# Source indices loaded once and copied into slots on chip, eight slots for gathered rows

## The reference

```
h  = relu(layernorm(x))
Q, K, V = h Wq + bq, h Wk + bk, h Wv + bv          (8 heads of 12)
Ee = edge_attr We + be
score(e) = exp(clip(sum over a head of K[src] * Q[dst] * Ee / sqrt(12), -5, 5))
x  = x + segsum(V[src] * score, dst) / (segsum(score, dst) + 1e-6)

h  = relu(layernorm(x))
m  = segsum(h[src], dst) / max(degree, 1)
y  = m Wl^T + bl + h Wr^T
x  = x + relu(batchnorm over all nodes(y))
```

## Time and profile before

| | |
|---|---|
| time, median of 3 runs | 4154.96 us (4154.8 to 4155.78) |
| span of the profiled execution | 5273.9 us |
| busy: PE, DVE, ACT, POOL | 2391.0, 1669.6, 365.5, 3049.5 us |
| gathers, stage 1 (L569) | 1564, mean 964 ns |
| gathers, stage 2 (L586) | 1564, mean 944 ns |

### The profile page before, as it was taken

The page is one execution under the profiler, slowest core; times in us unless marked ns, Lnnn a source line. Parts: engine busy times, 40 slices in busy tenths (PEclk is TensorE's granted clock), DMA queues, the critical chain, the costliest instruction groups (busy, mean ns, idle before and its releaser), DMA issues.

```text
span 5273.9 us, 63499 instructions
## 1 busy us (share of the span) xinstructions
PE 2391.0 (45%) x12016; PEld 2151.5 (41%) x12016; DVE 1669.6 (32%) x4551; ACT 365.5 (7%) x847; POOL 3049.5 (58%) x3199
## 2 busy tenths in 40 slices
PE   6555556555555565555553233333333333323332
PEld 4455555555555555555552222222222222222221
DVE  7344444444444444444442111111011111111114
ACT  5000100001000110001010000000000000000000
POOL 3555555555555555555554566665656666666564
PEclk9555555555555555555555555555555555555555
DMA  6444444444444444444441111111111111111112
GB/s 193 109 111 111 113 109 113 109 114 114 107 114 116 110 117 111 108 110 110 114 115 32 32 36 34 34 36 33 36 34 34 34 36 34 34 35 34 33 37 53
DMA packets 468836, 408.10 MB, mean 77 GB/s; under 512 B 279436, under 2 KB 380740, under 8 KB 468812
## 3 DMA queue, kind: packets, MB, share of 16 engines
q0 software_dynamic: 125120, 230.82, 18.8%
q1 hardware_dynamic: 317292, 164.73, 12.9%
q10 hardware_dynamic: 26400, 12.29, 0.8%
HBM read 380.19 MB, written 27.32 MB: 77 GB/s over the span
## 4 chain that ended last, share of the span: by engine, by line
another core or an unknown queue 34%; issue 22%; DVE 13%; DVEq 12%; PE 8%; DMA 4%; POOL 3%; SPq 2%; ACT 1%; POOLq 0%; ACTq 0%
DVEq L308 4%; DVE prod L1073 3%; POOL kvg L586 3%; DVEq L1011 3%; PE psum L667 3%; PE psum L751 2%; PE psum L676 2%; DMA kvg<-h_tab,idx 2%; DVE acc L1011 1%; DVE score L1078 1%; DMA idx<-in_src_dram 1%; DVE msg L1084 1%; DVE sel L1001 1%; DVE prod L1067 1%
## 5 line engine op out<-in xcount | busy, mean ns | idle before, releaser
L569 POOL DMA_INDIRECT kvg<-kv_tab,idx x1564 | 1507.7, 964 | 1142.4 <-issue 795.1
L586 POOL DMA_INDIRECT kvg<-h_tab,idx x1564 | 1476.3, 944 | 934.1 <-issue 502.4
L751 PE MATMUL psum<-sel,kvg 128*97 128x42 f32 x3136 | 583.2, 365 | 1382.4 <-DVE sel L1001 595.5
L751 PEld LDWEIGHTS psum<-sel,kvg 128*97 128x97 f32 x3136 | 533.2, 276 | 1454.4 <-issue 1066.7
L667 PE MATMUL psum<-sel,msg 128*104 128x42 f32 x3136 | 632.3, 381 | 789.6 <-DVE msg L1084 598.4
L667 PEld LDWEIGHTS psum<-sel,msg 128*104 128x104 f32 x3136 | 573.1, 288 | 869.5 <-DVE msg L1084 637.3
L1011 DVE TENSOR_TENSOR acc<-acc,psum 104x42 f32 (+1 forms) x784 | 156.2, 199 | 2423.4 <-remote 1433.7
L676 PE MATMUL psum<-we,ea_t 97*128 97x96 f32 x3136 | 837.1, 446 | 8.5 <-DMA ea_t<-in_edge_attr_dram 8.5
L676 PEld LDWEIGHTS psum<-we,ea_t 97*128 97x128 f32 x3136 | 771.8, 330 | 9.2 <-issue 9.2
L1067 DVE TENSOR_TENSOR prod<-kvg,psum 128x384 f32<-128x384 f32 x392 | 216.0, 551 | 566.8 <-remote 517.9
L683 PE MATMUL psum<-q_win,sel_t 126*128 126x96 bf16 x1568 | 202.7, 280 | 324.9 <-DVE sel_t L1056 199.1
(11 more groups left out here) (134 smaller groups left out, 1139.2 us busy)
## 6 DMA issues: line engine op xcount, KB each, us to landing
ea_t<-in_edge_attr_dram SPq DMA_DIRECT2D x392, 192.0 KB
dst_row<-rel_tab SPq DMA_DIRECT2D x392, 126.0 KB
kvg<-kv_tab,idx POOLq DMA_INDIRECT x1564
kvg<-h_tab,idx POOLq DMA_INDIRECT x1564
idx<-in_src_dram SPq DMA_DIRECT2D x782, 2.0 KB
kv_tab<-kvq_out SPq DMA_DIRECT2D x25, 384.0 KB, 2.5
q_win<-q_tab SPq DMA_DIRECT2D x392, 23.6 KB
q_tab<-q_out ACTq DMA_DIRECT2D x25, 288.0 KB, 2.4
```

What stands on the lines that cost most here:

```text
L569: pool.indirect_dma_start(out=kv_slot[k][:, t, :], out_offset=None, in_=kv_tab[:, :], in_offset=bass.IndirectOffsetOnAxis(ap=idx[:, k, t:t ...
L586: pool.indirect_dma_start(out=h1_slot[k][:, t, 0:D], out_offset=None, in_=h1_tab[:, :], in_offset=bass.IndirectOffsetOnAxis(ap=idx[:, k, t ...
L751: mm = pe.matmul(b_agg[k % 2][0:D + 1, 0:WIN], h1_slot[k][:, t, :], sel[:, k % 2, t, :], start=(t == 0), stop=(t == TILES - 1))
```

## The change

A constant `SLOTS = 2 * RING` (eight) is added. What was in four slots on the gather side, the gathered rows (`kv_slot`, `h1_slot`) and the indices (`idx`), is now in eight; `ea_t`, `dst_row`, `q_win` stay at four. `kv_slot` lies in the storage of `h_sb`, which is free in stage 1, `h1_slot` in a tensor of its own, in which `q_out` of the node stage lies too. SP loads all source indices into `idx_all` at the start, behind the four pieces of x and ahead of the last 84 rows of x. `idx_all` is 128 partitions x 400 batches x 4, and its source is cut into pieces of 16 bytes, as a partition takes 4 consecutive indices of a batch. The per-batch index loads of SP are gone in both stages. Instead ACT (stage 1) and DVE (stage 2) first copy the indices of batches 0 to 7 into the slots, and then, once the rows of batch b have been used, those of batch b + 8. POOL waits for these copies (`s_slot_idx`, `s_slot_idx1`) where it waited for the index DMAs. `s_msg` and `s_agg1` start at 8 instead of 4, so that POOL may be eight batches ahead. The innermost loop of every engine holds eight batches instead of four.

```diff
+SLOTS = 2 * RING
...
-        kvg = sb("kvg", [P, RING, TILES * KV])
-        idx = sb("idx", [P, RING, TILES], I32)
+        kv_slot = [h_flat[:, s * TILES * KV:(s + 1) * TILES * KV].rearrange("p (t f) -> p t f", f=KV) for s in range(SLOTS)]
+        h1g = sb("h1g", [P, SLOTS, TILES * (D + 1)])
+        idx_all = sb("idx_all", [P, NB + SLOTS, TILES], I32)
+        idx = sb("idx", [P, SLOTS, TILES], I32)
...
             def rings(g, i0, i1):
...
+                with eng.Fori(i0 // 2, i1 // 2) as i:
+                    m = i + g * (STRIDE // 2)
+                    for r in range(2):
+                        for k in range(RING):
+                            one(m * SLOTS + (RING * (r + 1) + k), k, m * 2 + (r + 1), RING * (1 - r) + k, m + r)
...
                 sp.dma_start(x_sb[:, t0:t1, :], tile_rows(t0, t1)).then_inc(s_x, 16)
+            sp.dma_start(idx_all[:, 0:WHOLE, :], src[0:WHOLE * ROWS].rearrange("(b p t) -> p b t", p=P, t=TILES)).then_inc(s_idx, 16)
+            sp.dma_start(idx_all[:, NB:NB + SLOTS, :],
+                         src[0:SLOTS * ROWS].rearrange("(b p t) -> p b t", p=P, t=TILES)).then_inc(s_idx, 16)
+            for b in range(WHOLE, NB):
+                if not only_repeats(b):
+                    sp.dma_start(idx_all[:, b, :], edges(src, b).rearrange("(p t) -> p t", t=TILES)).then_inc(s_idx, 16)
             sp.wait_ge(s_pool, PADDED)
             sp.dma_start(x_sb[0:REST, FULL, :], x[FULL * P:N, :]).then_inc(s_x, 16)
...
-                    for i in range(RING) if first else [0] if not isinstance(b, int) or b >= RING else []:
-                        sp.wait_ge(s_kq, n + 1 + i)
-                        if not only_repeats(b):
-                            sp.dma_start(idx[:, k + i, :], edges(src, b + i)
-                                         .rearrange("(p t) -> p t", t=TILES)).then_inc(s_idx[k + i], 16)
-                    sp.wait_ge(s_msg, n + 1)
+                    sp.wait_ge(s_msg, n + 1 + (SLOTS - RING))
...
-                    sp.wait_ge(s_agg1, n + 1)
-                    sp.dma_start(idx[:, k, :], edges(src, b).rearrange("(p t) -> p t", t=TILES)).then_inc(s_idx1[k], 16)
+                    return
...
+            made(pool.memset(idx_all[:, WHOLE + 1:NB, :], 0))
...
-                    pool.wait_ge(s_idx[k], gathers(k, w, j) * 16)
+                    pool.wait_ge(s_msg, n + 1)
                     pool.sem_inc(s_gate, 1)
-                    pool.wait_ge(s_msg, n + 1)
+                    pool.wait_ge(s_slot_idx, n + 1)
...
+            act.wait_ge(s_idx, 16 * IDX_LOADS)
+            act.wait_ge(s_pool, CLEARED)
+            nc.scalar.copy(idx[:, :, :], idx_all[:, 0:SLOTS, :]).then_inc(s_slot_idx, SLOTS)
...
                                          ACT.Exp).then_inc(s_exp, 1)
+                    nc.scalar.copy(idx[:, s, :].unsqueeze(1), idx_all[:, bass.ds(b + SLOTS, 1), :]).then_inc(s_slot_idx, 1)
...
+            dve.wait_ge(s_slot_idx, turns * NB + SLOTS)
+            nc.vector.tensor_copy(idx[:, :, :], idx_all[:, 0:SLOTS, :]).then_inc(s_slot_idx1, SLOTS)
...
+                def refill(b, s):
+                    nc.vector.tensor_copy(idx[:, s, :].unsqueeze(1),
+                                          idx_all[:, bass.ds(b + SLOTS, 1), :]).then_inc(s_slot_idx1, 1)
...
-                        add_sums(b - 1, (k - 1) % RING, w, n - 1, D + 1, s_agg1, RING, s_acc1)
+                        add_sums(b - 1, (k - 1) % RING, w, n - 1, D + 1, s_agg1, SLOTS, s_acc1)
+                        refill(b - 1, (s - 1) % SLOTS)
```

More of the change, by code:

```diff
@@ L75, in only_repeats, with gathers @@
         return isinstance(b, int) and repeated_partitions(b) == P
-    def gathers(k, w, j):
-        return w * sum(not only_repeats(b) for b in range(k, NB, RING)) + (j + 1)
+    def gathers(s, w, m):
+        return w * sum(not only_repeats(b) for b in range(s, NB, SLOTS)) + (m + 1)
     def repeated_partitions(b):
@@ L192, in graph_attention_then_sage_kernel @@
         s_dst_nat = sem("s_dst_nat")
-        s_idx = [sem(f"s_idx{k}") for k in range(RING)]
+        s_idx = sem("s_idx")
+        s_slot_idx = sem("s_slot_idx")
+        s_slot_idx1 = sem("s_slot_idx1")
         s_ea = [sem(f"s_ea{k}") for k in range(RING)]
@@ L296, in graph_attention_then_sage_kernel @@
         CONSTS = 13
-        PADDED, IOTAS, IDENTITY, ONE, ONE_ROWS, CLEARED = 1, 4, 6, 9, 13, 14
+        IDX_LOADS = 2 + sum(not only_repeats(b) for b in range(WHOLE, NB))
+        PADDED, IOTAS, IDENTITY, ONE, ONE_ROWS, CLEARED = 1, 4, 6, 9, 13, 15
         X_FIRST, X_LOADS = 7, 4
@@ L317, in edge_steps, with one @@
         def edge_steps(eng, w, step, in_order=None, midway=(), behind=()):
-            def one(b, k, j):
+            def one(b, k, j, s, m):
                 step(b, k, w * NB + b, w * RINGS + j,
-                     isinstance(b, int) and b == 0, isinstance(b, int) and b == NB - 1, j)
+                     isinstance(b, int) and b == 0, isinstance(b, int) and b == NB - 1, s, m)
             def rings(g, i0, i1):
[L328 to L331, removed]
+                with eng.Fori(i0 // 2, i1 // 2) as i:
[3 more added lines that the diff above has]
+                            one(m * SLOTS + (RING * (r + 1) + k), k, m * 2 + (r + 1), RING * (1 - r) + k, m + r)
             def between(stages, g):
@@ L569, in gather, with gather1 @@
                         pool.indirect_dma_start(
[L570 to L571 removed]
+                            out=kv_slot[s][:, t, :], out_offset=None, in_=kv_tab[:, :],
+                            in_offset=bass.IndirectOffsetOnAxis(
+                                ap=idx[:, s, t:t + 1], axis=0)).then_inc(s_kv[s], 16)
                 edge_steps(pool, w, gather)
             pool.wait_ge(s_acc0, 1)
[L575 to L577 removed]
+            for s in range(SLOTS):
+                pool.memset(h1_slot[s][:, :, D:D + 1], 1.0).then_inc(s_ones_col, 1)
+                pool.wait_ge(s_ones_col, s + 1)
             pool.wait_ge(s_h1st, 16 * (G + 1))
             with pool.Fori(0, passes(pool)) as w:
[L580 removed]
+                def gather1(b, k, n, turn, first, last, s, m):
                     if only_repeats(b):
                         return
[L583 removed]
+                    pool.wait_ge(s_slot_idx1, n + 1)
                     pool.sem_inc(s_gate, 1)
@@ L669, in aggregate, with step @@
                     mm.then_inc(s_agg, 1)
-                def step(b, k, n, turn, first, last, j):
+                def step(b, k, n, turn, first, last, s, m):
                     edge = ea_t[:, k, :].rearrange("c (p t) -> c t p", t=TILES)
@@ L740, in sum_group, with step1 @@
                 mm.then_inc(s_stat, 1)
-            pe.wait_ge(s_ones_col, RING)
+            pe.wait_ge(s_ones_col, SLOTS)
             pe.wait_ge(s_zero_ps, 1)
             with pe.Fori(0, turns) as w:
-                def step1(b, k, n, turn, first, last, j):
+                def step1(b, k, n, turn, first, last, s, m):
                     if not only_repeats(b):
-                        pe.wait_ge(s_h1g[k], gathers(k, w, j) * (16 * TILES))
+                        pe.wait_ge(s_h1g[s], gathers(s, w, m) * (16 * TILES))
                     pe.wait_ge(s_sel1, n + 3)
@@ L856, in _ @@
             with act.Fori(0, turns) as w:
-                edge_steps(act, w, lambda b, k, n, turn, first, last, j: None, in_order,
+                edge_steps(act, w, lambda b, k, n, turn, first, last, s, m: None, in_order,
                            midway=[(0, own_transposed)], behind=[(0, stage_and_square)])
```

57 lines of the change are left out of this document (29 added, 28 removed).

## The result

The changed kernel takes 4167.9 us (median, 4167.38 to 4169.19), the kernel before 4154.85 beside it: ratio 1.0032, 95% interval 1.0021 to 1.0042. It is slower, by 13 us, as forecast in sign; forecast were 36 us.

A forecast was written before the change was run, and what follows sets the result against it. POOL's back-to-back gathers were taken to bound the kernel. 4155.0 - 3 (slots, index loads) + 2.3 (start of stage 1) + 36.6 (load of all indices) = 4191 us, own range 4174 to 4210, 8 in 10 from 4130 to 4250.

The forecast's parts named there:

- POOL's pace bounds the kernel: Both gather stages: POOL sets the pace, gathers 1.25 us apart, 5.0 us a batch, at most some 6 us of stalls.
- The agreement within 6 us: Whole kernel: profiled span 5273.9 less POOL's waits inside the stages, 1124.5, gives 4149.4 us, close to the median 4155.0.
- Eight slots and index loads gone: Gather stages: removes what POOL waits for, not its own 5.0 us a batch; gain 0 to 5.6 us, taken as 3.
- Copies at 0: Gather stages: index copies by ACT (114 us) and DVE (70 us) are hidden behind POOL's gathers; cost 0.
- Start of stage 1, +2.3: Before the first gather: ACT's new copy into the slots delays it by 2.3 us, bounds 0 and 4.
- SP's load of all indices: Node stage: 51,072 packets ahead of the K/V stores take 50 us (36 to 64), making everything after 36.6 us later.
- lower bound of 11.2: Index load at the start: 11.2 ns per packet, from SP's queue in stage 2, gives at least 36 us.
- T - 13.4: Node stage: lateness in us of ACT's third `rows_out`, T being the index load's time; never made up afterwards.
- the upper bound: Index load at the start: at the 384-byte packets' rate, 796 per us, it takes at most 64 us.
- the faster one, real waits in the median: Gather stages: gathers take under 1.25 us unrecorded, POOL's waits are real; with 1.20 us, 4086 us; chance 0.2.
- The one with the load hidden: Node stage: packets go faster or K/V stores overtake them, loss under 10 us, time about 4157; chance 0.14.
- The slow one: Index load at the start: pieces stream at half the 384-byte packets' rate, 128 us, total 4269 us; chance 0.1.

The follow-up runs named there:

- e1: Kernel before plus an unused load of the 390 full batches of indices by SP at the start, which POOL awaits: 4168.21 us against 4147.96, ratio 1.0048.
- h1: Kernel before with only its four K/V slots moved into the storage of h_sb: 4147.15 us against 4146.69, ratio 1.0001.
- e7: The changed kernel itself, unaltered, run where before took 5276.1 us: 5270.18 us, ratio 0.9990.
- e3: Changed kernel with eight slots, but POOL at most four batches ahead: 4160.25 us against 4147.96 for before, ratio 1.0031.
- f5: Changed kernel with SP loading each batch's indices again in stage 2, without that stage's copies: 4158.39 us against 4146.13 for before, ratio 1.0031.
- f6: Changed kernel with SP loading each batch's indices again in stage 1, without that stage's copies: 4156.97 us against 4146.13 for before, ratio 1.0027.
- h2: Kernel before with only the innermost loops made eight batches long: 4150.87 us against 4146.69, ratio 1.0009.
- f7: The changed kernel itself, unaltered, run again where before took 4146.13 us: 4159.56 us, ratio 1.0032.
- e2: Changed kernel with the index load cut into pieces of 16 batches, one behind each K/V store: 4142.67 us against 4147.96 for before, ratio 0.9986.
- f8: Changed kernel with index pieces behind the K/V stores and first eight batches loaded straight into the slots: 4136.91 us against 4146.13 for before, ratio 0.9978.

## Why the prediction was wrong

*POOL's pace bounds the kernel.* Right. The gathers are 1.25 us apart with no other wait, in before (e1, h1) as in the changed kernel. That the median holds none of the 1124.5 us of waits was right too. The reason that I gave, that profiling makes them, was wrong: the same profiler found none in e1, and e7 shows them with the changed kernel. And the profiled span being hundreds of us shorter is no merit of the change: e7, the changed kernel in a profile of before's kind, has 5266.7. The agreement within 6 us was in part luck: the gap between two gathers is 0.305 us (953 us over 3126 gaps in e1), not 0.30, which makes 1110 us of waits and 4164, and the 9 us above the median are a gap between the stages and an end that are together 11 us longer in that profile than in e1.

*Eight slots and index loads gone: 0 to 5.6, taken as 3.* The waits gave 0 (e3, f5, f6). What the whole brought is 9 us of shorter issues in stage 1 and some 3 at the end, which I had no term for.

*Copies at 0.* Right for the stages (f5, f6). The doubled loop at 0 as well: POOL's gaps in stage 1 add up to 476.6 us in h2 and 476.9 in h1, so its turns neither cost nor save a gap.

*Start of stage 1, +2.3.* Right mechanism, too small, though inside its bounds of 0 and 4: 3.6 (f7 and f6, each against its last Q store). ACT's copy starts 2.2 us after its last Q store's issue, and POOL's gather 1.2 us after the copy; the second piece was missing.

*SP's load of all indices: this is the step that failed, by its size.* "I take the middle, 50 us": the stream took 29.9 us (27.6 to 57.5 us), and 9.3 ns per packet is below my lower bound of 11.2. The relation T - 13.4 gives 16.5 us for it; the third `rows_out` was 17.3 us late, and e1's first gather 18.4. So the path was right, and the first gather came at 142.94 us, not at 158. The relation is a little short: from the third `rows_out` to the last Q store a further 1.4 to 2.9 us are lost (e1, f5, f7), for which it has no term, and why is open.

T was 20 us too long. With 29.9 in its place the sum is 4155 - 3 + 2.3 + 16.5 = 4171, 3 us above the result. That closeness is luck: the start came 24.1 us late in f7 where those terms make 18.8, and stage 1 and the end gave back 12 where the sum has 3.

Two things went into the bad T. The lower bound was no bound: it was a mean over packets of different sizes (in those 2370 us the trace has 49,152 packets of 16 bytes at 8.0 ns each and 12,288 of 384 bytes at 23.7), and it took a packet's own time for the time from one packet to the next. In the stream these are 16.6 and 9.3 ns. And the upper bound was the rate of 384-byte packets: 6366 packets and 2.43 MB in 8 us are 304 GB/s, while the index stream has 28 GB/s. That those were limited by their bytes, and so said nothing of small ones, fits both rates; it is argued, as no run varied the packet size.

The Trainium skill (DMA: Bandwidth & Descriptors, section Bandwidth) gives about 10.5 ns a packet, for a transfer of 64 packets issued by GpSimd. Taken as the time per packet on each of 16 engines, an estimate, it makes 34 us. The runs have 9.3 ns and 29.9 us: near it, in another queue than the page's. That the 11.2 ns of the mixed queue agreed with the page was chance.

The rivals: the faster one, real waits in the median, is out by e1 and e3. The one with the load hidden is out as it stood, since the K/V stores wait behind the stream, but e2 and f8 show that the load can be hidden, by 24 stores that each leave room for a piece. The slow one is out by the 1723 packets per us.

## What to carry to other kernels

Before waits in one profile are counted as gain, hold its span against the median: where the span exceeds the median by about the sum of the waits, they belong to that execution, and removing their cause buys nothing in the median. A bulk load that replaces hidden small ones must itself be hidden: in a queue that other transfers share it delays whatever is issued behind it by its stream time, so cut it into pieces behind the transfers that matter. To time a stream of small packets look for the rate of small packets in a row, not for the rate of large ones and not for a packet's own time, since such times overlap.

## What the runs showed of the hardware that I had not expected

- 16-byte packets of one large DMA from HBM stream at 1723 per us in one queue, one every 9.3 ns on each of 16 engines, 28 GB/s, while each takes 16.6 ns; SP is held for 29.61 us in the issue of the small DMA behind it.
- With loops of eight batches more instructions are fetched: the instruction queue q14 moved 127 packets, 1.04 MB, in h2 (above), 118 of them in stage 1, and in h1, with loops of four, 8 in stage 1:

```profile
q14 instruction: 17, 0.14, 0.0%
```

  h2 is 4 us over before at the medians (1.0009, 1.0000 to 1.0018), which hardly differs from none; POOL's idle time before gathers is 479.6 us in h2 and 479.9 in h1, so POOL, which sets the pace, doesn't wait for the fetches.
